# The last head of an attention kernel: accumulator banks swapped, four score banks, one projection bank, and a new order of TensorE's work

## The reference, cut to what matters

```
xn  = layernorm(x)
z   = layernorm(xn) * g + b
q, v = z @ wq.T + bq, z @ wv.T + bv ;  k = q
att = softmax(q k^T / 4) v        per batch and head: 32 pairs of (batch, head), 2048 x 2048 scores each
out = x + (att @ w_out.T + b_out) + (gelu(xn @ T(W1).T + b1) @ T(W2).T + b2)      T: ternary weights
```

## Time and profile before

| | |
|---|---|
| median of 3 runs | 1406.39 us (1405.15 to 1406.46) |
| profiled execution, as a run | 1407.6 us |
| its span in the profile | 1406.0 us |
| busy, whole span | TensorE 1375.9, VectorE 1333.8, ScalarE 1242.5, GpSimd 120.0 us |
| granted TensorE clock, mean | 0.994 of full speed (2.4 GHz) |
| score matmuls of the last head (line 465) | 64, 12.7 us busy |
| PV matmuls of the last head (line 476) | 128, 17.0 us busy |
| projections (line 495) | 192 |
| last head's projection (line 505) | 32, 9.3 us busy |

### The profile page before, as it was taken

One profiled execution on the slowest core, in us unless ns is written; L12 is line 12 of the kernel. 1 busy time (PEld: TensorE's weight loads), 2 busy tenths in 40 slices (PEclk: granted clock), 3 DMA queues, 4 the chain that ended last, 5 costly groups with the idle time before them and its releaser, 6 DMA issues.

```text
span 1406.0 us, 32225 instructions
## 1 busy us (share of the span) xinstructions
PE 1375.9 (98%) x13382; PEld 444.8 (32%) x13382; DVE 1333.8 (95%) x1429; ACT 1242.5 (88%) x2276; POOL 120.0 (9%) x254
## 2 busy tenths in 40 slices
PE   7999999999999999999999999999999999999998
PEld 4656643222222222222222222222222222222244
DVE  6898999999999999999999999999999999999934
ACT  5564638999999999999999999899999999999975
POOL 2101033000000000000000000000222200001200
PEclk8999999999999999999999999999999999999999
DMA  6011000010000000001000000011111110001122
GB/s 237 27 41 62 31 17 1 32 31 32 32 32 32 32 32 32 32 32 32 32 32 32 31 31 34 26 34 43 55 55 55 51 34 32 32 33 62 40 103 82
DMA packets 28795, 60.69 MB, mean 43 GB/s; under 512 B 6272, under 2 KB 11808, under 8 KB 28394
## 3 DMA queue, kind: packets, MB, share of 16 engines
q1 hardware_dynamic: 28074, 56.99, 12.0%
q10 hardware_dynamic: 576, 1.65, 0.3%
HBM read 41.29 MB, written 16.77 MB: 41 GB/s over the span
## 4 chain that ended last, share of the span: by engine, by line
DVE 55%; PE 40%; issue 2%; ACT 1%; DMA 1%; POOL 0%; ACTq 0%; DVEq 0%; POOLq 0%
DVE part_max L895 53%; PE ps L397 14%; PE ps L416 8%; PE ps L360 6%; PE ps L1218 3%; PE ps L1135 3%; PE ps L1155 2%; PE ps L495 2%; PE ps L476 1%; DMA rows<-in_rows 1%; ACT w L1109 1%; PE ps L465 1%; PE ps L505 0%; PE ps L1190 0%; DVE weight_scratch L887 0%
## 5 line engine op out<-in xcount | busy, mean ns | idle before, releaser
L895 DVE TENSOR_REDUCE part_max<-ps 128x1 f32<-128x1024 f32 x1024 | 1165.8, 1215 | 4.7 <-PE ps L360 4.5
L1109 ACT ACTIVATE w<-ps 128x512 f32<-128x512 f32 x2048 | 1111.3, 595 | 63.4 <-PE ps L416 21.7
L397 PE MATMUL ps<-w,v_ones 128*32 128x256 f32 (+1 forms) x7688 | 627.8, 398 | 0.6 <-DVE resid L814 0.3
L416 PE MATMUL ps<-qry,key 50*128 50x512 f16 x1984 | 409.8, 387 | 7.3 <-ACT w L1109 7.1
L360 PE MATMUL ps<-qry,key 48*128 48x512 f16 x2048 | 403.5, 379 | 5.0 <-DVE part_max L895 5.0
L397 PEld LDWEIGHTS ps<-w,v_ones 128*32 128x32 f32 x7688 | 152.2, 108 | 380.1 <-issue 209.0
L416 PEld LDWEIGHTS ps<-qry,key 50*128 50x128 f16 x1984 | 100.6, 92 | 439.3 <-ACT w L1109 412.1
L360 PEld LDWEIGHTS ps<-qry,key 48*128 48x128 f16 x2048 | 101.4, 95 | 33.1 <-DVE part_max L895 14.6
L691 POOL COPY v_ones<-v_all 128x128 f32<-128x128 f32 x64 | 18.7, 293 | 746.8 <-PE ps L397 746.8
L1071 ACT ACTIVATE q_split<-q_by_factor,sigma_bq 128x512 f16<-128x512 f32 x16 | 11.1, 719 | 63.5 <-DVE q_by_factor L795 63.1
L1218 PE MATMUL ps<-x,w_ternary 128*128 128x512 f16 x256 | 61.9, 380 | 1.9 <-ACT hidden L1075 1.8
(11 more groups left out here) (152 smaller groups left out, 489.6 us busy)
## 6 DMA issues: line engine op xcount, KB each, us to landing
key<-q_parts SPq DMA_DIRECT2D x62, 128.0 KB
qry<-q_parts SPq DMA_DIRECT2D x62, 128.0 KB
o_heads<-o_evacuated SPq DMA_DIRECT2D x31, 256.0 KB, 9.9
key<-q_parts SPq DMA_DIRECT2D x66, 64.0 KB
qry<-q_parts SPq DMA_DIRECT2D x66, 64.0 KB
resid<-in_x SPq DMA_DIRECT2D x8, 512.0 KB, 13.6
q_parts<-q_split SPq DMA_DIRECT2D x16, 256.0 KB, 2.3
out<-resid SPq DMA_DIRECT2D x7, 512.0 KB, 3.2
```

What stands on the lines that cost most here:

```text
L397: mm = eng.matmul(pv[32 * c:32 * c + 2 * D, c0:c1], vst[:, kb, :], prob[kb % 2][:, c * BANK + c0:c * BANK + c1], start=(kb == 0), stop=(kb ...
L416: eng.matmul(ring_bank(v, i, False), key[v][r:r + KROWS, kb * P:(kb + 1) * P], qry[v][r:r + KROWS, c * BANK:(c + 1) * BANK], start=True, s ...
L895: dve.tensor_reduce(part_max[h % 2][:, blk, side:side + 1], pa[a % 2], AX.X, ALU.max).then_inc(s_r, 1)
L1109: act.activation(prob[kb % 2][:, c * BANK:(c + 1) * BANK], ring_bank(k, i, last), ACT.Exp, scale=exp_scale).then_inc(s_e, 1)
```

## The change

The PSUM banks of the last head are given out anew: PV groups use banks 0 and 6 in turn (0 first) instead of 6 and 0; the projections use bank 2 alone; the scores rotate over four banks 3, 7, 4, 5, and a chunk waits for the exponential four before it. In each block the four chunks come in a row, then the PV block, then the projections. In block 15 the order is chunks, PV block 14, first half of projection 15, `project_last` 10 and 11, PV block 15, second half of projection 15, `project_last` 12 to 15. VectorE's queue follows: in block 15 `add_last` 10 and 11 go ahead of `add_y(15)`. `project(n, 0)` now waits for the addition of projection n-1. The first PV block waits for no evacuation any more; the one of group 1 waits for head 30's.

```diff
--- before.py
+++ after.py
@@ -228,9 +228,10 @@
         pa = [bank(0, 2), bank(2, 2)]
         pb = [bank(4), bank(5), bank(7)]
         pv = bank(6)
-        pv_last = [bank(6), bank(0)]
-        py = [bank(2), bank(3)]
-        pl = [bank(1)] * (3 * TG) + [bank(4), bank(5), bank(7), bank(6)]
+        pv_last = [bank(0), bank(6)]
+        py = bank(2)
+        pb_last = [bank(3), bank(7), bank(4), bank(5)]
+        pl = [bank(1)] * (3 * TG) + [bank(4), bank(5), bank(7), bank(3)]
 
 
 
@@ -369,7 +370,9 @@
         assert ROT * TURNS % len(pb) == 0
 
         def ring_bank(k, i, last):
-            return pb[(TURNS * k + i + (i >= MAX_AT and not last)) % len(pb)]
+            if last:
+                return pb_last[i % len(pb_last)]
+            return pb[(TURNS * k + i + (i >= MAX_AT)) % len(pb)]
 
         def max_bank(k):
 
@@ -460,7 +463,7 @@
             kb, c = i % NBLK, i // NBLK
             if i == 0:
                 eng.wait_ge(s_mr, 32 * (h + 1))
-            eng.wait_ge(s_e, NE * h + i - len(pb) + 1)
+            eng.wait_ge(s_e, NE * h + i - len(pb_last) + 1)
             r = tile(i)
             eng.matmul(ring_bank(v, i, True), key[v][r:r + KROWS, kb * P:(kb + 1) * P],
                        qry[v][r:r + KROWS, c * BANK:(c + 1) * BANK], start=True, stop=True).then_inc(s_b, 1)
@@ -470,8 +473,8 @@
             eng.wait_ge(s_e, NE * h + NCH * (n + 1))
             if n == 0 or n == 2:
                 eng.wait_ge(s_vs, 2 * h + 1 + n // 2)
-            if k0 == 0:
-                eng.wait_ge(s_o, h + max(0, c - 1))
+            if k0 == 0 and c:
+                eng.wait_ge(s_o, h + c - 1)
             for j in range(NCH):
                 mm = eng.matmul(pv_last[c % 2][32 * j:32 * j + 2 * D, :], vst[:, k0 + j, :],
                                 prob[n % 2][:, j * BANK:(j + 1) * BANK], start=(k0 == 0), stop=(k0 == NBLK - NCH))
@@ -488,11 +491,11 @@
                 else:
                     eng.wait_ge(s_on, 3 * (NT0 + g - NCH + 1))
                     eng.wait_ge(s_kn, g - NCH + 1)
-                wait(eng, s_yd, n - 1)
+                wait(eng, s_yd, n)
             terms = [(k, a, b) for k in range(KC) for a, b in ((0, 0), (1, 0), (0, 1))]
             for m, (k, a, b) in enumerate(terms):
                 rows = HR if g >= NCH and k else P
-                mm = eng.matmul(py[n % 2][:, j * C:(j + 1) * C], o_parts(g, k)[0:rows, a, t * P:(t + 1) * P],
+                mm = eng.matmul(py[:, j * C:(j + 1) * C], o_parts(g, k)[0:rows, a, t * P:(t + 1) * P],
                                 wop[0:rows, b, k, :], start=(m == 0), stop=(m == len(terms) - 1))
             if j:
                 mm.then_inc(s_y, 1)
@@ -508,21 +511,23 @@
             eng.wait_ge(s_r, NA * NH)
             eng.wait_ge(s_wl, 16 * 2 * NCH)
             for n in range(NBLK):
-                for j in range(2):
+                for j in range(NCH):
                     last_chunk(eng, NCH * n + j)
                 if n:
                     pv_block(eng, n - 1)
                 else:
                     for x in range(2):
                         pv_half(eng, NH - 2, NBLK - 1, x)
-                for j in range(2, NCH):
-                    last_chunk(eng, NCH * n + j)
-                for j in range(2):
-                    project(eng, n, j)
-                for m in last_at(n):
-                    project_last(eng, m)
-            pv_block(eng, NBLK - 1)
-            for m in last_at(NBLK):
+                project(eng, n, 0)
+                if n == NBLK - 1:
+                    for m in last_at(n) + last_at(NBLK)[:1]:
+                        project_last(eng, m)
+                    pv_block(eng, n)
+                project(eng, n, 1)
+                if n < NBLK - 1:
+                    for m in last_at(n):
+                        project_last(eng, m)
+            for m in last_at(NBLK)[1:]:
                 project_last(eng, m)
 
         NPC = 4
@@ -969,7 +974,7 @@
                 dve.wait_ge(s_y, n + 1)
                 dve.wait_ge(s_xb, n // 2 + 1)
                 wait(dve, s_ld2, lasts)
-                dve.scalar_tensor_tensor(out=r, in0=py[n % 2].rearrange("p (t c) -> p t c", c=C), scalar=yun[:, 0:1], in1=r,
+                dve.scalar_tensor_tensor(out=r, in0=py.rearrange("p (t c) -> p t c", c=C), scalar=yun[:, 0:1], in1=r,
                                          op0=ALU.mult, op1=ALU.add).then_inc(s_yd, 1)
 
             def normalise_rest(j):
@@ -993,15 +998,20 @@
 
             lasts = 0
             for n in range(NBLK):
+                if n == NBLK - 1:
+                    for m in last_at(n) + last_at(NBLK)[:1]:
+                        add_last(m, n)
+                        lasts += 1
                 add_y(n, lasts)
                 if n == 0:
                     recip(2)
                 if NCH <= n < 2 * NCH:
                     normalise_rest(n - NCH)
-                for m in last_at(n):
-                    add_last(m, n + 1)
-                    lasts += 1
-            for m in last_at(NBLK):
+                if n < NBLK - 1:
+                    for m in last_at(n):
+                        add_last(m, n + 1)
+                        lasts += 1
+            for m in last_at(NBLK)[1:]:
                 add_last(m, NBLK)
 
         @block.scalar
```

## The result

The changed kernel takes **1410.14 us** in the median of 18 runs (1407.55 to 1411.45), the kernel before 1406.41 (1405.15 to 1409.08). The ratio is 1.0022 with a 95% interval of 1.0015 to 1.0028: slower by 3.1 us (0.22%), or 3.7 by the medians. The forecast was 1407.6, no change that can be told. The median of 1410.14 is 0.2 us above the upper end of its range, 1409.9; by the ratio to the kernel before, which makes 1409.5 of the forecast's base of 1406.39, it is inside. It lies where the forecast put its rival A: the stall before projection 2 came as worked out, and TensorE's clock fell in it.

A forecast was written before the change was run, and what follows sets the result against it. The last head's stage was taken as bound by TensorE's order of work, with one hole. The terms +1.78 - 1.3 + 0.1 + 0.9 - 0.3 gave +1.2 us, a median of 1407.6 us, range 1405.7 to 1409.9.

The forecast's parts named there:

- rival A: Stall before projection 2: TensorE's clock falls to half, losing 2.0 us, total +3.2, 1409.6 us; chance 0.12.
- step 1: Blocks 0 to 1: swapped accumulators spare the first PV block its wait for bank 6; projection 1 comes 1.43 us earlier.
- step 2: Block 2: with one bank, projection 2 waits for projection 1's addition behind recip(2); TensorE stands 3.3 us, 1.78 us later.
- step 3: Blocks 2 to 15: four scores in a row save one tile-shape change, 0.10 us per block, 1.3 us in all.
- Rival C: Each block's shape change from PV block to projection costs nearly its upper bound: +3.1 us, 1409.5 us; chance 0.06.
- The estimate of 0.053 us: Per block, a tiling-mode change priced as a drain of about 128 cycles; 13 blocks would save 0.7 us, not 1.3.
- 1.3 - 0.1: Blocks 2 to 15: 1.3 us saved by fewer tile-shape changes, less 0.1 for line 505's late wait in blocks 5 to 8.
- step 4: Block 15 and the end: the last additions finish 0.9 us later, and the last store gives 0.3 us back.
- The 0.3 that the last store was to give back: End of span: with an emptier queue ahead, the last store's landing may fall from 2.1 towards 1.8 us.
- the sign that the forecast had named for A: TensorE after the stall before projection 2: a granted clock below 1.00 after 1354 us.
- Rival B: Block 2: projection 2 does not stand because recip(2) comes earlier; -2.2 us, 1404.2 us; chance 0.06.

The follow-up runs named there:

- experiments 4 to 6: Kernel before with accumulators swapped alone, 1406.36 us; with four normalise_rest moved to blocks 6, 8, 10 and 12, 1406.44 us; with both, 1405.02 us.
- Experiment 1: Changed kernel with recip(2) queued behind the addition of projection 1 instead of projection 0: 1406.49 us, ratio to the kernel before 1.0001.
- experiment 4: Kernel before with the PV accumulators swapped alone, two projection banks kept: 1406.36 us, ratio 0.9999.
- experiment 10: Changed kernel with recip(2) and normalise_rest moved later, two banks at the end, and scores split two before, two behind the PV block: 1404.89 us.
- experiment 9: Changed kernel with TensorE's and VectorE's order of block 15 taken back to that of the kernel before: 1409.29 us.
- experiment 3: Changed kernel with four filler matmuls, result not read, ahead of projection 2: 1409.68 us, ratio to the kernel before 1.0019.

## Where the prediction was right, and where it failed

**Swap (step 1): right.** 1.43 forecast from projection 0 to 1, 1.44 measured (4.39 to 2.95), and the PV block waits for nothing. What I did not see is that it was worthless by itself: experiments 4 to 6 show that the next wait, of the first normalise_rest for its loads, takes it. With the stall in front, that wait never showed.

**One bank (step 2): right.** Projection 2 was forecast 9.23 after projection 0 (1354.20 against 1344.97) and came 9.16 after it, released by the line of additions. The idle time is 3.19, forecast 3.3. It takes two things: the DMA wait of recip(2) ahead of the addition, and the single bank. Experiment 1 has the single bank without that wait ahead of projection 1's addition, experiment 4 the wait with two banks, and in neither does TensorE stand before projection 2. Two banks in the changed kernel were not tried.

**Four in a row (step 3): right.** Blocks of 2.95 and 3.39, and 3.55 behind two of the normalisations; PV block to projection is 1.00 (1363.11 to 1364.11), so the missing transition costs what a PV block to scores does. Rival C is out. The estimate of 0.053 us, from the drain that the Trainium skill gives on its page TensorE: Matmul & The Clock Gate, Step-by-step: what each phase is for, was too low by half: experiment 10 measures 0.10. From projection 2 to 15, less the 2.7 us of the clock, it is 43.1 us instead of 44.3: 1.2 won, forecast 1.3 - 0.1.

**The end (step 4): right but for one term.** +0.9 forecast, 0.88 measured, 0.85 by experiment 9. The 0.3 that the last store was to give back did not come: from the last addition to the end of the span it is 2.43 us in both profiles. The 2.1 us of the earlier trace rows was the median of the four 128 KB stores; the last of them alone landed in 1.8 before, and in 1.8 after. The median did fall to 1.8, but the span ends with the last. This term was mis-sized; its measure is 0.0.

**The clock: the step that failed.** The sum put the clock behind the stall at nothing, and left it to rival A, with a chance of 0.12 and a price of 2.0 us. In the profile the clock fell, the sign that the forecast had named for A, and by times and mean clocks it probably did in most of the 18 runs. Its price there is the 5.48 of block 2 and the 3.14 of block 3 less twice 2.95, **2.7 us**, the largest term of all; in experiments 3 and 9 it was 1.6. The argument was that the 3.3 us "lies nearer to the long ones" of the earlier trace rows, which should have made A likely; against it stood only that no shorter gap had been seen to do it. That the median still came within 0.2 us of the range is owed to A's place in it, not to the forecast. Here the fall came about 2.3 us after TensorE ran dry (1349.3 to 1351.6), and experiment 3 shows it with a gap of 2.2. The Trainium skill's page TensorE: Matmul & The Clock Gate, Why this matters for your kernels, warns of idle gaps between bursts; this trace agrees, with 3.19 us idle and a granted clock of 0.50 behind it.

**Sum.** As measured, projection 2 came 1.7 later (9.16 instead of 1352.42 - 1344.97 = 7.45), and 1.7 - 1.2 + 0.9 + 0.0 + 2.7 = +4.1 us; the stage grew by 65.1 - 61.0 = 4.1. The medians grew by 3.7. Rival B (no stall, because recip(2) comes earlier) did not come: the load of the sums was issued 4.93 us after the start of projection 0 and 4.94 before. Experiment 1, without the stall, has a stage of 61.2 us and not 2.2 below 61.0, but there recip(2) and the loads behind it are not earlier, so it does not say what B would have given.

## What to carry to other kernels

When a second buffer is taken away, look at what stands ahead of the releasing instruction in its engine's queue: here a bank that the steady blocks did not need was what kept TensorE clear of a DMA wait in VectorE's queue. A hole that is removed may be the cover of the next wait, so name that next wait and move both. A stall of TensorE of the size seen here has to be priced with the low clock behind it: 1.6 to 2.7 us on top of stalls of 2.2 to 3.2 us.

## What I had not expected of the hardware

In the three traces of the last head in which TensorE was idle for 2.16 to 3.19 us (experiment 3, experiment 9 and the changed kernel) the granted clock fell, during the idle time or just after it. Run times suggest that it does not in every execution: two of the changed kernel's 18 are as short as without it. An idle time of 1.26 us before and of 1.06 us in experiment 1 left it at 1.00. The same stall did not cost the same: in the changed kernel's profile the clock was low from about 1351.6 to 1358.4, 5.9 us of that work, and 2.7 us were lost; in experiment 9, with 3.14 us idle, it fell only about 0.1 us before TensorE started again, and 1.6 us were lost.
